# A graph transformer layer with a mixture of experts: factor products paired by weight unit, routed sums carried in PSUM by ScalarE, the second turn moved, and the graph sum split in two parts

## The chip, the cores and the metric

The kernel runs on one core of one Trainium2 chip. The metric is the device time of one execution in microseconds. A core's engines each run their own instructions in a fixed order and meet by semaphores: TensorE (PE) multiplies, VectorE (DVE) and ScalarE (ACT) work element by element, GpSimd (POOL) issues a few gathers, SyncE (SP) issues the loads of the weights.

## The reference, cut to what matters

```python
xn = layernorm(x)                                  # x: 625 x 1024
h = xn @ W; e = exp(-leaky_relu(al[src] + ar[dst]))
gnn = elu(segment_sum(e * h[dst], src) / (segment_sum(e, src) + 1e-5))
mix = linear_attention(xn, w_qkv, w_out, b_out)    # 16 heads, elu + 1 kernel
x = x + gnn + mix
y = layernorm(x)
# 8 experts, top 2, capacity 97 tokens, inner width 4096
eout = (silu(xg @ rg[e]) * (xg @ ru[e])) @ rd[e]   # for each expert e
shared = (silu(y @ sg) * (y @ su)) @ sd            # inner width 8192
x = x + shared + scatter(eout * weight)
```

All is float32.

## The kernel before

Every float32 product is made of three matmuls in the fp32r format: an operand a is split into a_hi (a rounded copy, ScalarE, `hi(u)`) and a_lo = a - a_hi (VectorE, `lo(u)`), and hi*hi, lo*hi and hi*lo are summed in a PSUM bank (`three`). A weight unit is a tile of 128x1024; hi and lo parts of units go round a ring of seven.

A first part (some 480 us) does the edge counts, the layer norm, h, the graph sum (`agg_ps`, in plain float32: 5x5x2 matmuls of the edge weights C by h, with a row sum behind them), Q, K, V, the attention and its output. Then come 32 steps for the experts' layer, four (q=0..3) for each expert e. Each step takes a quarter of the expert's inner width and 1/32 of the shared layer's. The step e=0 q=0 has an order of its own (FIRST), so has e=7 q=3 (LAST); the 30 others are STEP.

A STEP has 35 units. Units 0 to 6 are the factors of a seven-product (Strassen-like) scheme for the shared gate and up weights, in the order A11, S3, S2, A12, S1, A22, S4; S factors are sums of raw blocks that VectorE makes (L1139 to L1149). Each factor is multiplied by tokens in two column tiles j=0, 1 (`product(j, i)`, 12 matmuls of 314 columns). Units 7 to 14 are the routed gate and up weights of half b=0 (`routed_up(0)`), 15 to 18 the shared down weights, 19 to 26 routed half b=1, 27 to 34 the routed down weights (`routed_down(k0, k1)`). The shared down units are multiplied by a seven-product scheme too (`shared_down_products`): P1A, P1B, TA, TB (the last token tile, two triples each), P7A, P7B, P6A, P6B, P2A, P2B, P5A, P5B, P4A, P4B, P3A, P3B, 18 triples in all. They read sh_hi/lo and hs_hi/lo, which are made from the shared inner values: `shared_up`, `shared_mult`, `inner_sums`, `inner_lo`, `inner_sums_lo`; and `down_sums` makes sums of the raw down weights. Partial products that more than one result needs are copied from bank to bank by ScalarE (`down_seed`, L907) and results are added to `resid` by VectorE (`down_add`, L1605).

The routed inner values of half b (`silu_routed(b)` on ScalarE, `routed_inner(b)` on VectorE, L1534, into r_h) are transposed on TensorE (`turn_inner(b)`), split (`turned_hi`, `turned_lo`, L1615) and read by routed_down. The result of a step's eight down units stands in banks R0 and R0+1 and is added to `eout` by VectorE in the next step (`routed_add`, L1493), between the two column tiles' products. At q=0 the next expert's tokens, gathered by GpSimd (`xg`, issued behind the second turn of q=3, since it shares memory with r_h), are transposed (`turn_expert`) and split (`tokens_hi`, `tokens_lo`).

The orders on the engines are written out by hand. ScalarE, GpSimd and SyncE loop over the experts 1 to 6, TensorE and VectorE are unrolled. `kept` and `choice_row` (L1471 to L1483) make the positions and weights for the final sum from the routing.

Of the kernel before, what the change touches and what calls it, by code (L numbers as in the profile page):

```python
# [35 lines left out]
LOW_SBUF = DMA_SCRATCH + 128  # L36
P = 128
# [41 lines left out]
T_BANK = (A0 + 1, A0)  # L79
# [14 lines left out]
AGG_BANK = (7, 0, 1, 2)  # L94
# [24 lines left out]
class Order:  # L119


    def __init__(self, s, gate, sd, rd, a_bank, seq=tuple(range(NPROD)), banks=BANKS, paired=False, sd_units=2):
# [3 lines left out]
        self.down_before, self.after_down = (1, 3) if sd_units == 4 else (0, 1) if s < sd < gate[0] else (None, 0)  # L126
        self.a_bank, self.seq, self.banks, self.paired = a_bank, seq, banks, paired
# [31 lines left out]
    def raw(self, u):  # L159
        if self.shared(u):  # L160
            i = self.seq[u - self.s]
            return SPARE if self.paired and i == F_S2 else self.b0 + FACTOR_RAW[i]
        return self.block(u)
# [7 lines left out]
STEP = Order(s=0, gate=(7, 19), sd=15, rd=27, a_bank=(A0, X0), sd_units=4)  # L171
# [6 lines left out]
def build(nc, x, src, dst, W, a, w_qkv, w_out, b_out, router_w, rg, ru, rd, sg, su, sd, out):  # L178
# [27 lines left out]
    cursor[0] = max(cursor[0], 16512)  # L206
# [149 lines left out]
    assert here() <= early_at  # L356
# [139 lines left out]
    def _(sp):  # L496
# [60 lines left out]
    def _(pool):  # L557
# [15 lines left out]
        link(nc.gpsimd.memset(p7[:], 0.0))  # L573
# [24 lines left out]
        pool.wait_ge(sem("agg_ps"), 2 * NT)  # L598
        nc.gpsimd.memset(vv[:, :, :, P:VW], 1.0).then_inc(sem("v_ones"), 1)
# [50 lines left out]
    def _(act):  # L650
# [94 lines left out]
        for i in range(4):  # L745
            w_part(G_K + 1, i)
        for t in range(NT):
# [3 lines left out]
        for dt in range(NT):  # L751
# [3 lines left out]
            nc.scalar.activation(zt[dt % 2][:], zt[dt % 2][:], ACT.Exp, scale=-1.0).then_inc(sem("ez_done"), 1)  # L755
        for t in range(NT):
# [72 lines left out]
        def step(e, q, order=STEP):  # L829
# [66 lines left out]
            def down_seed(n):  # L896
# [5 lines left out]
                if n in (2, 3):  # L902
                    act.wait_ge(sem("sd_added"), count(e, q, 2 * NT, (2, 1)[n - 2] + ONE))
# [4 lines left out]

            def tokens_hi(half):
                act.wait_ge(sem("xgT_ps"), e * 2 + (half + 1))  # L910
                nc.scalar.copy(xgT_hi[:, half * 4 * CAP:(half + 1) * 4 * CAP],
                               PS[A0 + half][:, 0:4 * CAP]).then_inc(sem("xg_hi"), 1)

            if order is LAST:
                for u in range(15):
# [67 lines left out]
            for u in range(4):  # L983
                hi(u)
            shared_seeds(0, (), (4,), (5,), (6,))
# [3 lines left out]
            shared_seeds(1, (7,), (8,), (9,), (10,), (11, 12), (13,))  # L989
# [1336 lines left out]
```

## Time and profile before

| | |
|---|---|
| median of 3 runs | 2950.28 us (2948.54 to 2950.53) |
| profiled execution | 2947.98 us, of which the span is 2946.2 |
| TensorE busy | 2802.9 us, 95% |
| VectorE busy | 2431.4 us, 83% |
| ScalarE busy | 1659.4 us, 56% |
| TensorE's granted clock, mean | 0.999 of full speed |

The span goes from the first instruction to the last; the rest of the profiled execution's time lies around it. The TensorE clock is given in shares of its full 2.4 GHz. A plain step (q above 0) takes 76.18 us, and an expert of four steps 306.45.

### The profile page before, as it was taken

To read this page: it belongs to the slowest core of one execution; us is meant where nothing else is said; L and a number is where in the kernel's file an instruction comes from. 1 tells how busy PE (TensorE), PEld (TensorE's weight loads), DVE (VectorE), ACT (ScalarE), POOL (GpSimd) and SP (SyncE) were. 2 spreads that over 40 slices of the span, in tenths; PEclk is the share of its full clock that TensorE was granted. 3 is DMA by queue.
4 is the path that set the end of the run, shared out by engine and by line. 5 is a ranking of instruction groups with operands and counts; after the bars stand their busy time and mean duration, and the time that the engine had idled before them with its cause. 6 is when DMAs were issued, how large, how long until landed. Compare 5 with 4: busy or idle time off the path is not lost.

```text
span 2946.2 us, 41411 instructions
## 1 busy us (share of the span) xinstructions
PE 2802.9 (95%) x14706; PEld 2273.9 (77%) x14706; DVE 2431.4 (83%) x3069; ACT 1659.4 (56%) x2271; POOL 57.2 (2%) x74
## 2 busy tenths in 40 slices
PE   9999999999999999999999999999999999999998
PEld 8875898777777777777777777777777777777777
DVE  8756258988888888888888888888888888888888
ACT  7621224555665656655665556655666555556663
POOL 1100000000000000000000000000000000000001
PEclk9999999999999999999999999999999999999999
DMA  3111122666666666665766666666666666666676
GB/s 110 37 57 58 58 72 92 219 207 212 207 212 210 214 212 217 206 213 182 225 208 200 207 219 206 202 206 220 214 208 207 213 204 204 208 219 206 206 247 229
DMA packets 270279, 549.08 MB, mean 186 GB/s; under 512 B 16673, under 2 KB 82465, under 8 KB 269927
## 3 DMA queue, kind: packets, MB, share of 16 engines
q1 hardware_dynamic: 265954, 532.11, 55.7%
q0 software_dynamic: 3936, 14.06, 1.5%
q8 instruction: 117, 1.92, 0.3%
q14 instruction: 110, 0.90, 0.1%
q10 hardware_dynamic: 162, 0.08, 0.0%
HBM read 537.49 MB, written 8.70 MB: 185 GB/s over the span
## 4 chain that ended last, share of the span: by engine, by line
PE 67%; DVE 20%; ACT 6%; issue 5%; DMA 0%; ACTq 0%; DVEq 0%; POOL 0%; POOLq 0%; SPq 0%
PE ps L2042 18%; PE ps L2046 17%; PE ps L2045 17%; DVE c_lo L1508 6%; ACT c_hi L839 4%; PE ps L1810 3%; DVE c_lo L1156 3%; PE ps L1847 2%; PE ps L1849 2%; PE ps L1848 2%; PE ps L1900 1%; DVE raw L1143 1%; DVE raw L1146 1%; DVE raw L1139 1%; ACT c_hi L719 1%
## 5 line engine op out<-in xcount | busy, mean ns | idle before, releaser
L1508 DVE TENSOR_TENSOR c_lo<-raw,c_hi 128x1024 fp32r<-128x1024 f32 x892 | 1054.2, 1217 | 128.4 <-ACT c_hi L839 128.2
L839 ACT CAST c_hi<-raw 128x1024 fp32r<-128x1024 f32 x892 | 894.7, 1047 | 260.5 <-DVE raw L1594 146.9
L2042 PE MATMUL ps<-tok_hi,c_hi 128*128 128x314 f32 x1792 | 558.2, 312 | 51.4 <-DVE c_lo L1156 49.4
L2046 PE MATMUL ps<-tok_hi,c_lo 128*128 128x314 f32 x1792 | 552.0, 308 | 0.0
L2045 PE MATMUL ps<-tok_lo,c_hi 128*128 128x314 f32 x1792 | 552.0, 308 | 0.0
L2042 PE MATMUL ps<-c_hi,xgT_hi 128*97 128x512 f32 x1024 | 406.4, 397 | 0.0
L2046 PE MATMUL ps<-c_hi,xgT_lo 128*97 128x512 f32 x1024 | 403.1, 394 | 0.0
L2045 PE MATMUL ps<-c_lo,xgT_hi 128*97 128x512 f32 x1024 | 402.8, 393 | 0.0
L2042 PEld LDWEIGHTS ps<-tok_hi,c_hi 128*128 128x128 f32 x1792 | 339.3, 189 | 71.4 <-DVE c_lo L1156 43.0
L2045 PEld LDWEIGHTS ps<-tok_lo,c_hi 128*128 128x128 f32 x1792 | 339.8, 190 | 0.1
L2046 PEld LDWEIGHTS ps<-tok_hi,c_lo 128*128 128x128 f32 x1792 | 338.2, 189 | 0.0
L719 ACT CAST c_hi<-raw 128x1024 fp32r<-128x1024 f32 x224 | 230.7, 1046 | 147.8 <-DVE raw L1143 84.0
L1156 DVE TENSOR_TENSOR c_lo<-raw,c_hi 128x1024 fp32r<-128x1024 f32 x224 | 269.8, 1221 | 25.8 <-ACT c_hi L719 24.8
L2042 PE MATMUL ps<-c_hi,hT_hi 128*97 128x512 f32 x512 | 206.4, 403 | 35.1 <-DVE hT_lo L1615 35.1
L2042 PEld LDWEIGHTS ps<-c_hi,xgT_hi 128*97 128x97 f32 x1024 | 166.2, 162 | 73.0 <-issue 9.0
L2046 PEld LDWEIGHTS ps<-c_hi,xgT_lo 128*97 128x97 f32 x1024 | 166.2, 162 | 70.8
L2045 PEld LDWEIGHTS ps<-c_lo,xgT_hi 128*97 128x97 f32 x1024 | 166.3, 162 | 64.2
L2046 PE MATMUL ps<-c_hi,hT_lo 128*97 128x512 f32 x512 | 202.3, 395 | 0.0
L2045 PE MATMUL ps<-c_lo,hT_hi 128*97 128x512 f32 x512 | 201.2, 393 | 0.0
L1605 DVE TENSOR_TENSOR resid<-ps,resid 125x512 f32<-125x512 f32 x300 | 189.1, 676 | 0.0
L883 ACT CAST hT_hi<-ps 128x388 fp32r<-128x388 f32 x64 | 30.6, 478 | 238.0 <-PE ps L2093 238.0
L2042 PEld LDWEIGHTS ps<-c_hi,hT_hi 128*97 128x97 f32 x512 | 82.9, 162 | 86.9 <-DVE hT_lo L1615 42.3
(274 smaller groups left out, 4047.5 us busy)
## 6 DMA issues: line engine op xcount, KB each, us to landing
raw<-in_L_ffn_rg SPq DMA_DIRECT2D x256, 512.0 KB, 4.9
raw<-in_L_ffn_ru SPq DMA_DIRECT2D x256, 512.0 KB, 4.3
raw<-in_L_ffn_rd SPq DMA_DIRECT2D x256, 512.0 KB, 4.8
raw<-in_L_ffn_sg SPq DMA_DIRECT2D x64, 512.0 KB, 5.5
raw<-in_L_ffn_su SPq DMA_DIRECT2D x64, 512.0 KB, 6.3
raw<-in_L_ffn_sd SPq DMA_DIRECT2D x64, 512.0 KB, 4.3
wl<-in_L_mix_w_qkv SPq DMA_DIRECT2D x6, 2048.0 KB, 8.0
wl<-in_L_gnn_W SPq DMA_DIRECT2D x2, 2048.0 KB, 22.2
```

The lines of the kernel that those rows point to most:

```text
L719: nc.scalar.copy(c_hi[u % RING][:], raw_at_(q, r)[:]).then_inc(sem("hi_done"), 1)
L839: nc.scalar.copy(c_hi[u % RING][:], raw_at_(q, r)[:]).then_inc(sem("hi_done"), 1 + (U - order.units) * (u == order.units - 1))
L1156: V.tensor_tensor(c_lo[u % RING][:], raw_at_(q, r)[:], c_hi[u % RING][:].bitcast(F32), ALU.subtract).then_inc(sem("lo_done"), 1)
L1508: V.tensor_tensor(c_lo[u % RING][:], raw_at_(q, r)[:], c_hi[u % RING][:].bitcast(F32), ALU.subtract).then_inc(sem("lo_done"), 1 + (U - ord ...
L1605: V.tensor_tensor(r, PS[bank][0:TP, :], r, ALU.add).then_inc(sem("sd_added"), 1)
L1810: m = MM(PS[dt][0:TP, 0:SC], oh_d[slot(gr, c)][:, dt * TP:(dt + 1) * TP], oh_s[slot(gr, c)][:, 0:SC], start=(c == 0), stop=(c == EG - 1))
L1847: MM(ps, l_hi[:, k, ts], hi[:, i, :], start=(k == 0), stop=False)
L1848: MM(ps, l_hi[:, k, ts], lo[:, i, :], start=False, stop=False)
L1849: m = MM(ps, l_lo[:, k, ts], hi[:, i, :], start=False, stop=(k == KT - 1))
L2042: m = MM(out_, l_hi, r_hi, start=first, stop=False, skip_group_check=skip)
L2045: MM(out_, l_hi, r_lo, start=False, stop=False, skip_group_check=skip)
L2046: return MM(out_, l_lo, r_hi, start=False, stop=last, skip_group_check=skip)
```

## The change

1. STEP's factor products are paired by unit: product(0,i), product(1,i), with four banks for j=1 (R0, R0+1, A0, A0+1). At q=0 the tokens are transposed before the products, and split between them.
2. `routed_add` goes. ScalarE copies the banks into `eout` (`routed_out`) after hi(3), and at q>0 copies `eout` back into the banks (`routed_seed`) after hi(26), so that routed_down sums onto it.
3. The last token tile is treated alike: `last_seed` puts resid into banks 7 and 4, `last_out` takes it out; two VectorE additions go.
4. The hand-written orders of VectorE and ScalarE are changed: `down_sums` and c_lo(15), c_lo(16) stand ahead of `inner_sums_lo`; the down seeds and the additions come earlier among the units; `routed_inner(1)` after lo(32).
5. The second turn comes after two down units instead of four, in bank X0+3.
6. The graph sum uses split operands: 150 matmuls in fp32r instead of 50 in float32, with C_hi and h_hi by ScalarE and C_lo and h_lo by VectorE; a row sum bank, one weight load and a memset are moved for it, and parts of the K and V weights are prepared at other places.
7. `kept` and `choice_row` move from FIRST to the step e=0 q=1, after lo(8).
8. LAST: `routed_out` after hi(5) instead of the additions.

```diff
-T_BANK = (A0 + 1, A0)
+T_BANK = (A0 + 1, X0 + 3)
...
-AGG_BANK = (7, 0, 1, 2)
+AGG_BANK = (7, 6, 1, 2)
+ROWSUM_BANK = 5
...
-STEP = Order(s=0, gate=(7, 19), sd=15, rd=27, a_bank=(A0, X0), sd_units=4)
+STEP = Order(s=0, gate=(7, 19), sd=15, rd=27, a_bank=(A0, X0), banks=((X0, X0 + 1, X0 + 2, X0 + 3), (R0, R0 + 1, A0, A0 + 1)),
+             paired=True, sd_units=4)
...
+        def row_hi(t):
+            act.wait_ge(sem("h_out"), NT + t + 1)
...
+            nc.scalar.copy(h_hi[t][:], h[:, t, :]).then_inc(sem("h_hi_out"), 1)
...
+            def last_seed(half):
+
+                act.wait_ge(sem("sd_added"), count(e, q, 2 * NT, ONE))
+                act.wait_ge(sem("s_up"), count(e, q, 4, 4 + ONE))
+                act.wait_ge(sem("t4_out"), count(e, q, 2, 0))
+                act.wait_ge(sem("silu_done"), count(e, q, 6, 1))
+                nc.scalar.copy(PS[DOWN_LAST[half]][0:TP, :],
+                               resid[:, NT - 1, half * HALF:(half + 1) * HALF]).then_inc(sem("t4_seeded"), 1)
+
+            def last_out(half):
+
+                act.wait_ge(sem("down_ps"), count(e, q, 16, (D_TA, D_TB)[half]))
+                nc.scalar.copy(resid[:, NT - 1, half * HALF:(half + 1) * HALF],
+                               PS[DOWN_LAST[half]][0:TP, :]).then_inc(sem("t4_out"), 1)
+
+            def routed_out(half):
+
+                act.wait_ge(sem("unit_used"), count(e, q, U, USED0))
+                act.wait_ge(sem("eout_clear"), e + (1 if q == 0 else 2))
+                nc.scalar.copy(eout[:, half * HALF:(half + 1) * HALF],
+                               PS[R0 + half][0:CAP, :]).then_inc(sem("rd_added"), 1)
+
+            def routed_seed(half):
+
+                act.wait_ge(sem("rd_added"), count(e, q, 2, half + 1))
+                act.wait_ge(sem("sd_added"), count(e, q, 2 * NT, (6, 8)[half] + ONE))
+                nc.scalar.copy(PS[R0 + half][0:CAP, :],
+                               eout[:, half * HALF:(half + 1) * HALF]).then_inc(sem("eout_seeded"), 1)
...
             if order is LAST:
-                for u in range(15):
+                for u in range(6):
+                    hi(u)
+                routed_out(0)
+                routed_out(1)
+                for u in range(6, 15):
                     hi(u)
...
-            for u in range(4):
-                hi(u)
-            shared_seeds(0, (), (4,), (5,), (6,))
+            hi(0)
+            hi(1)
             if q == 0:
                 tokens_hi(0)
                 tokens_hi(1)
-            shared_seeds(1, (7,), (8,), (9,), (10,), (11, 12), (13,))
+            hi(2)
+            hi(3)
+            routed_out(0)
+            routed_out(1)
...
             inner_sums_hi()
-            for u in range(15, 17):
-                hi(u)
+            hi(15)
+            hi(16)
+            last_seed(0)
+            last_seed(1)
             silu_routed(0)
-            for u in range(17, 22):
-                hi(u)
+            hi(17)
+            hi(18)
             down_seed(0)
             down_seed(1)
-            hi(22)
-            for n in range(2, 6):
-                down_seed(n)
-            for u in range(23, 30):
+            hi(19)
+            last_out(0)
+            last_out(1)
+            down_seed(2)
+            down_seed(3)
+            hi(20)
+            down_seed(4)
+            down_seed(5)
+            for u in range(21, 27):
                 hi(u)
+            if q == 0:
+                act.sem_inc(sem("eout_seeded"), 2)
+            else:
+                routed_seed(0)
+                routed_seed(1)
+            hi(27)
+            hi(28)
+            silu_routed(1)
+            hi(29)
             turned_hi(0)
-            silu_routed(1)
-            for u in range(30, 32):
+            for u in range(30, 35):
                 hi(u)
             turned_hi(1)
...
+            V.tensor_tensor(C_lo[:, dt, :], Cf[:, dt, :], C_hi[dt][:].bitcast(F32),
+                            ALU.subtract).then_inc(sem("C_lo_out"), 1)
...
                 lo(order.s + F_S3)
+                if tokens:
+                    tokens_lo(0)
+                    tokens_lo(1)
                 sums(F_S2)
...
             if order is LAST:
-                for u in range(6):
+                for u in range(15):
                     lo(u)
-                routed_add(count(e, q, U, USED0), cleared)
-                for u in range(6, 15):
-                    lo(u)
...
-                        kept()
-                    if u > 20:
-                        choice_row(u - 21)
...
-            factors()
-            routed_add(count(e, q, U, USED0), cleared)
-            shared_up(0)
-            shared_mult(0)
-            if q == 0:
-                tokens_lo(0)
-                tokens_lo(1)
+            factors(tokens=q == 0)
             for u in range(7, 12):
                 lo(u)
+                if e == 0 and q == 1 and u == 8:
+                    kept()
+                    choice_row(0)
+                    choice_row(1)
+            shared_up(0)
+            lo(12)
             shared_up(1)
-            lo(12)
+            shared_mult(0)
             shared_mult(1)
             inner_sums()
             lo(13)
             inner_lo(0)
             inner_lo(1)
             lo(14)
+            lo(15)
+            lo(16)
+            down_sums()
             inner_sums_lo()
-            for u in range(15, 17):
-                lo(u)
-            down_sums()
+            lo(17)
             routed_inner(0)
-            for u in range(17, 20):
-                lo(u)
-            down_add(DOWN_LAST[0], D_TA, NT - 1, 0)
-            lo(20)
-            down_add(DOWN_LAST[1], D_TB, NT - 1, 1)
+            lo(18)
+            lo(19)
             p7_add(0)
             p7_add(1)
+            lo(20)
+            for p in range(2):
+                down_add(DOWN_B[p], (D_P2A, D_P2B)[p], 2 * p, 0, 1 if p else 3)
             lo(21)
-            for p in range(2):
-                down_add(DOWN_B[p], (D_P2A, D_P2B)[p], 2 * p, 0)
-            lo(22)
             for p in range(2):
                 dve.wait_ge(sem("down_seeded"), count(e, q, 6, 5 + p))
                 down_add(DOWN_A[p], (D_P5A, D_P5B)[p], 2 * p + 1, 1)
+            lo(22)
...
-            for u in range(23, 30):
+            for u in range(23, 29):
                 lo(u)
             turned_lo(0)
+            for u in range(29, 33):
+                lo(u)
             routed_inner(1)
-            for u in range(30, 32):
-                lo(u)
+            lo(33)
+            lo(34)
             turned_lo(1)
...
             for dt in range(NT):
-                m = MM(PS[AGG_BANK[j % 4]][0:TP, :], Cf[:, dt, t * TP:(t + 1) * TP],
-                       h[:, dt, half * HALF:(half + 1) * HALF], start=(dt == 0), stop=(dt == NT - 1))
+                MM(ps, C_hi[dt][:, ts], h_hi[dt][:, cols], start=(dt == 0), stop=False)
+                MM(ps, C_hi[dt][:, ts], h_lo[:, dt, cols], start=False, stop=False)
+                m = MM(ps, C_lo[:, dt, ts], h_hi[dt][:, cols], start=False, stop=(dt == NT - 1))
...
+                seeded = order is STEP and q > 0
...
+                    if k == 0 and seeded:
+                        pe.wait_ge(sem("eout_seeded"), count(e, q, 2, 2))
...
+                    pe.wait_ge(sem("t4_seeded"), count(e, q, 2, half + 1))
...
-            products(0)
             if q == 0:
                 turn_expert()
-            pe.wait_ge(sem("rd_added"), count(e, q, 2, 2))
-            products(1)
+            for i in order.seq:
+                if i == F_S3 and q == 0:
+                    pe.wait_ge(sem("xgT_ready"), e * 2 + 1)
+                product(0, i)
+                if i == F_A11:
+                    pe.wait_ge(sem("rd_added"), count(e, q, 2, 1))
+                if i == F_S3 and q == 0:
+                    pe.wait_ge(sem("xgT_ready"), e * 2 + 2)
+                product(1, i)
...
             turn_inner(0)
             routed_up(1, (1,))
-            routed_down(0, 4)
+            routed_down(0, 2)
             pe.wait_ge(sem("h_done"), count(e, q, 2, 2 + ONE))
             turn_inner(1)
-            routed_down(4, 8)
+            routed_down(2, 8)
```

## Rows read from the trace of the kernel before

**Rows 1.** The page's part 1: busy time, share of the span and instructions.

```profile
PE 2802.9 (95%) x14706; PEld 2273.9 (77%) x14706; DVE 2431.4 (83%) x3069; ACT 1659.4 (56%) x2271; POOL 57.2 (2%) x74
```

**Rows 2.** Waits of TensorE: engine, line, releaser: total us, times, longest.

```profile
PE ps L2042 <- DVE c_lo L1156: 49.4, 58, 1.7
PE ps L2042 <- DVE hT_lo L1615: 35.1, 30, 1.2
PE ps L2042 <- ACT ps L907: 34.7, 30, 1.2
```

**Rows 3.** Windows: us, busy of PE, PEld, DVE, ACT, POOL, clock, DMA share, GB/s.

```profile
2174.77:2250.95 76.18, 72.33 (x374) 58.12 (x375) 65.78 (x75) 45.75 (x60) 0.00 (x0) 1.00 0.64 208
2174.77:2200.82 26.05, 24.74 (x169) 24.49 (x169) 20.30 (x21) 15.09 (x22) 0.00 (x0) 1.00 0.52 168
2211.94:2250.95 39.01, 36.47 (x159) 25.79 (x158) 34.45 (x40) 23.90 (x29) 0.00 (x0) 1.00 0.70 227
481.00:484.00 3.00, 3.00 (x14) 3.00 (x13) 2.22 (x2) 0.83 (x2) 0.00 (x0) 0.51 0.02 6
```

**Rows 4.** Timeline of TensorE in the plain step: start, us, instruction, idle before.

```profile
2179.79 0.38 PE L2042 MATMUL ps<-tok_hi,c_hi 128*128 128x314 f32 x1 [1.31 <-DVE c_lo L1156]
```

**Rows 5.** The page's part 5: busy us, mean ns of one, idle before.

```profile
L1508 DVE TENSOR_TENSOR c_lo<-raw,c_hi 128x1024 fp32r<-128x1024 f32 x892 | 1054.2, 1217 | 128.4 <-ACT c_hi L839 128.2
L839 ACT CAST c_hi<-raw 128x1024 fp32r<-128x1024 f32 x892 | 894.7, 1047 | 260.5 <-DVE raw L1594 146.9
```

**Rows 6.** Timeline of VectorE in the plain step.

```profile
2202.11 0.81 DVE L1552 TENSOR_TENSOR s_up<-s_up,s_gate 128x628 f32<-128x628 f32 x1
...
2214.15 0.68 DVE L1534 TENSOR_TENSOR r_h<-ps,r_h 97x512 f32<-97x512 f32 x1
...
2225.15 3.67 DVE L1605 TENSOR_TENSOR resid<-ps,resid 125x512 f32<-125x512 f32 x6
2228.74 8.02 DVE L1508 TENSOR_TENSOR c_lo<-raw,c_hi 128x1024 fp32r<-128x1024 f32 x7
```

**Rows 7.** Timeline of ScalarE in the plain step.

```profile
2201.02 0.43 ACT L869 ACTIVATE s_gate<-ps 128x314 f32<-128x314 f32 x1 [0.71 <-PE ps L2046]
...
2218.12 1.06 ACT L907 COPY ps<-ps 125x512 f32<-125x512 f32 x2
```

**Rows 8.** Timelines of GpSimd, TensorE, ScalarE and VectorE at the start of e=6.

```profile
2319.95 0.18 POOL L629 COPY tok_cur<-tok_u 97x1 uint32 x1 [277.31 <-PE ps L2093]
2320.97 0.97 POOL L604 DMA_INDIRECT xg<-y_rows,tok_cur  x1 [0.83 <-POOL tok_cur L629]
...
2328.60 0.38 PE L2042 MATMUL ps<-tok_hi,c_hi 128*128 128x314 f32 x1 [1.73 <-DVE c_lo L1156]
...
2342.83 0.87 ACT L911 CAST xgT_hi<-ps 128x388 fp32r<-128x388 f32 x2
...
2343.69 1.02 DVE L1621 TENSOR_TENSOR xgT_lo<-ps,xgT_hi 128x388 fp32r<-128x388 f32 x2
```

**Rows 9.** DMA issues, 2310 to 2340: median us from issue to landing.

```profile
xg<-y_rows,tok_cur POOLq DMA_INDIRECT x1, 8.1
```

**Rows 10.** Groups of TensorE, 236.8 to 281.1: busy us, mean ns of one.

```profile
L1900 PE MATMUL ps<-h,C 125*125 125x512 f32 x100 | 43.3, 593 | 0.0
```

**Rows 11.** Timelines of TensorE and VectorE in FIRST and in LAST.

```profile
542.91 0.18 DVE L1471 TENSOR_SCALAR rt_keep<-rt_rank 125x40 f32<-125x40 f32 x1
...
545.46 0.19 DVE L1477 TENSOR_TENSOR rt_t<-rt_oh,rt_keep 125x40 f32<-125x40 f32 x1
...
550.41 0.55 PE L2093 MATMUL ps<-ident,r_h 97*128 97x97 f32 x4 [2.93 <-DVE r_h L1534]
...
2867.21 1.28 DVE L1493 TENSOR_TENSOR eout<-ps,eout 97x512 f32<-97x512 f32 x2
...
2882.26 0.30 PE L2093 MATMUL ps<-ident,r_h 97*128 97x97 f32 x1 [2.94 <-DVE r_h L1534]
```

**Rows 12.** Timeline of TensorE at the start of FIRST.

```profile
480.25 0.41 PE L2042 MATMUL ps<-tok_hi,c_hi 128*128 128x314 f32 x1 [1.98 <-DVEq L1777]
```

More of the change, by code:

```diff
@@ L36 @@
 LOW_SBUF = DMA_SCRATCH + 128
+RESID_AT = 16512
 P = 128
@@ L161, in raw @@
             i = self.seq[u - self.s]
-            return SPARE if self.paired and i == F_S2 else self.b0 + FACTOR_RAW[i]
+            return SPARE if self.paired and self.sd_units == 2 and i == F_S2 else self.b0 + FACTOR_RAW[i]
         return self.block(u)
@@ L746, in _ @@
             w_part(G_K + 1, i)
+        def row_hi(t):
+            act.wait_ge(sem("h_out"), NT + t + 1)
+            if t == 3:
+                act.wait_ge(sem("biased"), NT)
+            nc.scalar.copy(h_hi[t][:], h[:, t, :]).then_inc(sem("h_hi_out"), 1)
+        for t in range(4):
+            row_hi(t)
         for t in range(NT):
@@ L755, in _ @@
             nc.scalar.activation(zt[dt % 2][:], zt[dt % 2][:], ACT.Exp, scale=-1.0).then_inc(sem("ez_done"), 1)
+        act.wait_ge(sem("w_lo"), w_parts(G_K + 3, 3))
+        act.wait_ge(sem("albc_ps"), 2)
+        for dt in range(NT):
+            act.wait_ge(sem("ez_used"), dt + 1)
+            nc.scalar.copy(C_hi[dt][:], C[:, dt].rearrange("p c two -> p (c two)")).then_inc(sem("C_hi_out"), 1)
+        row_hi(NT - 1)
         for t in range(NT):
@@ L1218, in k_map @@
             feature_map(half * NT + t, ps, TP, HALF, kk[:, t, half * HALF:(half + 1) * HALF])
-            if t < 4:
+            if g is not None and t < 4:
                 w_part(g, t)
@@ L1251, in _ @@
         edge_weights(NT - 1)
-        for t in range(NT):
-            k_map(1, t, G_V)
+        dve.wait_ge(sem("ez_used"), NT)
         csum = zt[1]
@@ L2074, in product @@
                     pe.wait_ge(sem("silu_done"), count(e, q, 6, order.silus(1, 0)))
-                elif i == F_S3 and j == 1:
+                elif i == F_S3 and j == 1 and order is LAST:
                     pe.wait_ge(sem("silu_done"), count(e, q, 6, order.silus(0, 1)))
@@ L2133, in routed_down @@
                         m = three(PS[R0 + half][0:CAP, :], hT_hi[:, xs], hT_lo[:, xs],
-                                  c_hi[u % RING][:, c], c_lo[u % RING][:, c], k == 0, k == 7)
+                                  c_hi[u % RING][:, c], c_lo[u % RING][:, c], k == 0 and not seeded, k == 7, skip=seeded)
                     m.then_inc(sem("unit_used"), 1 + (U - order.units) * (u == order.units - 1))
```

126 lines of the change are left out of this document (91 added, 35 removed).

## The prediction

> **What bounds the kernel now.** I read the page first. TensorE is busy 95% of the span and VectorE 83% [rows 1], so the kernel is near the bound of its matmuls, and what a change of order can win is TensorE's idle time plus matmuls taken away. The list of what TensorE waited for says where that idle time is: three waits that come back in nearly each of the 30 STEP steps, behind a factor's low part (L1156), the seed copies (L907) and the low part of the second turn (L1615) [rows 2]. The windows of one plain step, e=5 q=2 from 2174.77 to 2250.95, give its length, 76.18, split at the starts of routed_up(0) (R, 2200.82) and of the shared down products (D, 2211.94) [rows 3]. The timeline of TensorE puts a number on the first: 1.31 idle before F_S2 [rows 4]; the waits' totals over 30 steps give 1.16 before P6A and 1.17 before the fifth routed_down unit [rows 2]. Counted from start to start, with the slower first matmul after a stall, they cost 1.46, 1.32 and 1.17, with 0.38 at the step's start and 0.15 of small ones: 4.48 a step. TensorE's own work is thus 71.7 and VectorE has 10.4 of slack [rows 3], but both run in a fixed order, so slack in the mean says little. The reader should follow chains.
>
> Durations that I use are pitches: a c_lo shows 1.217 but seven in a row take 8.02, so 1.14 each; six adds take 3.67, so 0.60 each [rows 5, 6]; a c_hi is 1.047, some 0.95 in a row [rows 5]. A product phase of 168 matmuls takes 26.05 less its stalls, 24.2, so one of the 14 products is 1.73 [rows 3]. The 150 matmuls of 512 columns after D, 36.5 of busy time with 8 transposes [rows 3], give 0.233 each, 0.70 for a triple and 1.40 for a routed unit of two.
>
> **Products paired by unit (30 steps).** TensorE now takes 3.46 for a unit's two products. VectorE needs a sum and a c_lo for the next one, 1.2 + 1.14. The stall before F_S2 and that at the start go: the product phase is 24.3 instead of 26.05, 1.8 less. The two additions of routed_add leave VectorE (1.2) and become ScalarE copies behind c_hi(3). Before shows no copy from SBUF to PSUM, and the nearest rows for all new copies are the PSUM-to-PSUM copy of L907, two in 1.06 [rows 7], 0.53 each; twice that is the other bound. I take 0.55. routed_out(0) is then done some 0.3 before product(1,A11) asks for its bank: nothing, but a thin margin. If it is late, it costs its lateness in 23 steps.
>
> **The wait before the shared down products.** This is what the old profile hides. They wait for inner_sums_lo, which in the old order came before c_lo(15), c_lo(16) and the four down_sums. In the new one it comes after all of them. The same instructions, from the multiplication at 2202.11 to the r_h at 2214.15, took 12.04 in an unbroken chain [rows 6]. The new chain starts when the last silu is done, R+0.66 (0.43 of silu after the last product and two hand-overs, [rows 7]), so hs_lo ends at R+12.7 and TensorE starts at about R+12.85, where its 48 matmuls end at R+11.12. A new stall of 1.7.
>
> **Inside the shared down.** P6A's stall goes (last_seed and the seeds move to where ScalarE is free). But down_seed(2) and (3) wait for P6A and P6B, the tenth triple, D+7.0, and c_hi(20) is behind them: ready at D+9.2; c_lo(20) ends at D+10.4, the P2 additions at D+11.6, c_lo(21) and P5A's addition at D+13.4. routed_up(1) needs that addition and wants to start at D+12.6: a stall of 0.75. TA's and TB's additions leave VectorE (1.2); last_seed and last_out (four copies of 0.55) lie on ScalarE, which is busy 45.8 of 76.18.
>
> **Second turn earlier.** turn_inner(1) moves from the fifth to the third unit of routed_down. It needs routed_inner(1), and VectorE has from c_lo(21) on no gap: 12 c_lo (13.6), 6 additions (3.6), hT_lo (0.5) and the multiplication (0.65), 18.4 in all, so from D+11.6 it ends at D+30.0. In the old step the same stretch, six additions from 2225.15 and then seven c_lo, was also unbroken [rows 6]. TensorE wants the turn at D + 12.6 + 0.75 + 11.2 + 0.44 + 2.8 = D+27.8. Stall 2.3 less what the modelled starts hide, 2.2. The old stall of 1.17 before the fifth unit goes.
>
> Sum of a plain step: stalls of 0.07 + 1.7 + 0.75 + 2.2 = 4.7 against 4.48. By ends: R at 24.3, D at R+12.85, the rest 38.95, 76.1; by stalls 76.4. I take +0.1, so +2 over the 23 steps with q>0.
>
> **The steps with q=0 (7).** The tokens of the next expert are gathered by a chain that starts with the second turn of q=3: the copy of the index list at 2319.95, the gather's issue at 2320.97 [rows 8] and its landing 8.1 after that [rows 9], so 9.1 from the copy and, with the turn and the hand-over ahead of the copy, 9.9 from the turn. The new turn is 8.8 before the step's end, the old one about 7.5 (the next step's first product would have been ready at about 2326.7), but the old step used the tokens only after 12 us of products; the new one turns them before its first product. They land 9.9 after D+30.1, 1.1 after the step's end at D+38.9. From the landing X: transposes 0.61, tokens_hi (0.87 for two) and tokens_lo (1.02 for two [rows 8]) to X+2.1, the F_S2 sum behind them to X+3.3, c_hi(2) and c_hi(3) behind that to X+5.2, routed_out(0) to X+5.85, and product(1,A11), ready at X+2.4, waits till X+6.0: 3.5. With the landing, restarts and the first c_lo 5.4 more than work, less the old start stall of such a step, 1.73 [rows 8], which these waits cover: +3.7. Less for the last expert, 1.1. Sum +26. The addition of part 7 to the one step e=0 q=1, 4.46 of VectorE, lies in the slack ahead of the last products, 0 to 1.
>
> **Prologue.** 50 fp32 matmuls, recorded as 100, take 43.3 [rows 10], 44.2 with the row sum. 150 fp32r matmuls of 512 columns at 0.233 and the row sum, 1.0, are 36.1. Their low parts are ready near 232.3, TensorE arrives at 236.89. −8.1; bounds 0 (operands late by so much) and −8.5.
>
> **FIRST and LAST.** The 4.46 of kept and choice rows go (542.91 to 544.32, and two rows of 1.5 such as that from 545.46) from ahead of the r_h whose turn stalls 2.93 in FIRST [rows 11]: −3.1, and −1.1 at the second turn. In LAST the stall is 2.94 behind c_lo, two eout additions (1.28 for two) and four more; the eout additions go [rows 11]: −1.2 at least, −3.7 if both stalls go; I take −2.5.
>
> **Sum.** +2 + 26 − 8.1 − 4.2 − 2.5 = +13. The profiled execution took 2947.98 (span 2946.2), so 2961; the runs' median lies 2.3 above it, so 2963.
>
> **A rule of the clock, weighed.** TensorE's granted clock was 0.51 (the level of 1.2 GHz) in 481.00 to 484.00, right after it had idled 1.98 before 480.25 with transposes ahead; the first products there ran at 0.26 a matmul instead of 0.145, about 1.5 lost [rows 3, 12]. After idles of 2.93 and 2.94 with dense work on either side [rows 11] it did not fall. The Trainium skill ("TensorE: Matmul & The Clock Gate", Part 1) says that idleness puts the array back to 1.2 GHz. By that rule each q=0 step would lose such a stretch again; by the rows at 550.41 it would lose nothing.
>
> **Rivals.** (1) Faster: VectorE's chains are not as tight as I add them up. If the order of arrival lets hs_lo end before R+11.1 (1.7 earlier), 30 steps give −51, 2912; if only the tail chain is shorter by 2.2, −66, 2897; it decides from 0.5 less stall a step on (−15 against +13 gives 2948; 0.7 gives 2942, on the other side). For it: VectorE has 2.4 less to do a step. Against it: the 12.04 was measured. 0.27 with the lower end of my own forecast. (2) The clock falls in the q=0 steps, whose idles of 1.1 and 3.5 are parted by transposes and one product: 7 × 1.5 = +10, 2973. 0.12. (3) The thin margin of routed_out and the seeds fails, a copy at twice its price: 0.5 in 23 steps, +12, 2975. 0.13. (4) Stalls only move and the q=0 wait is half hidden, since the gather lands earlier or ScalarE comes sooner to c_hi(3): +13 − 13, 2950. 0.15 by itself.
>
> **How the numbers follow.** My forecast, 2963, own range 2953 to 2972, has 0.33. A measurement of this kernel tells no change from within 0.2%, 5.9: faster is below 2944.4, slower above 2956.2. Faster takes rival 1, 0.27. Same takes rival 4 and the low end of mine, 0.18. Slower is the rest, 0.55. The range goes down to 2925, which leaves about half of rival 1 out, and up to 2982.
>
> **What would show it.** In a plain step: no gap before F_S2; a gap of 1.5 to 1.9 before the first shared down matmul behind L1583's hs_lo; 0.5 to 1 at the start of routed_up(1); about 2 before the r_h transposes of the second turn, behind r_h; a step of 76.1 to 76.4. In a q=0 step: a gap before the token transposes behind the gather and one of about 3.5 before product(1,A11) behind eout's copy. Aggregation 36 instead of 44. I am wrong if plain steps come out at 75 or less, then at D or at the turn; or if the second gap at q=0 is under 1.

## The result and the profile after

The changed kernel takes 2999.3 us (median of 4 runs, 2997.16 to 3001.31) against 2950.23: 1.0167 of the time before, 95% interval 1.0150 to 1.0185. It is slower, by 49, where 13 were forecast, and lies above the range. The profiled execution took 3001.31, its span is 2999.7.

The page, part 1, and the list of TensorE's waits:

```profile
PE 2816.5 (94%) x14756; PEld 2313.1 (77%) x14756; DVE 2372.0 (79%) x2957; ACT 1799.7 (60%) x2509; POOL 67.8 (2%) x74
```

```profile
PE ps L2163 <- issue: 71.2, 60, 2.0
PE ps L2214 <- DVE r_h L1660: 62.8, 32, 2.1
PE ps L2163 <- ACT eout L960: 20.6, 8, 3.5
PE ps L2225 <- issue: 14.4, 7, 3.2
```

The three waits of [rows 2] are gone, and four others stand there. The first row holds two of them (60 times in 30 steps), which the timeline of TensorE in a plain step (from 949.43) parts:

```profile
986.71 0.48 PE L2163 MATMUL ps<-c_hi,sh_hi 128*125 128x512 f32 x1 [1.62 <-issue]
...
1000.27 0.45 PE L2163 MATMUL ps<-c_hi,xgT_hi 128*97 128x512 f32 x1 [0.74 <-issue]
...
1016.77 0.56 PE L2214 MATMUL ps<-ident,r_h 97*128 97x97 f32 x4 [2.01 <-DVE r_h L1660]
```

From start to start they cost 1.78, 0.90 and 2.18, 4.86 in all, where the prediction had 1.7, 0.75 and 2.2. But two neighbouring steps with the same waits are not equally long. Windows (us, busy time of PE, PEld, DVE, ACT and POOL, TensorE's clock, DMA share, GB/s):

```profile
873.42:949.43 76.01, 71.60 (x376) 58.19 (x375) 61.97 (x69) 49.43 (x68) 0.00 (x0) 1.00 0.63 207
949.43:1027.04 77.61, 73.24 (x376) 59.15 (x375) 65.06 (x73) 51.27 (x70) 0.00 (x0) 0.98 0.61 204
1017.50:1020.50 3.00, 3.00 (x10) 1.92 (x9) 3.00 (x4) 1.29 (x2) 0.00 (x0) 0.55 1.08 369
1113.50:1116.50 3.00, 3.00 (x14) 3.00 (x13) 2.32 (x2) 1.83 (x3) 0.60 (x1) 0.50 0.42 132
```

The first is a step as forecast, 76.01 against 76.18 before [rows 3]. The second is 1.6 longer because TensorE works at half clock for some 3.5 us behind its second turn. The fourth row shows the same at q=0, behind the wait for the old rows' copy. Going through the span in windows of 1 us, and counting busy time by the missing share of the clock, there are 26 such stretches with 43.9 us lost in them; the kernel before has one, with 1.7. Of the 26, 15 come right behind a second turn with 2.0 of idle, 3 behind the wait for the gathered tokens, 7 behind the wait for the old rows' copy and 1 behind the wait for hs_lo.

At q=0 (timelines of GpSimd and TensorE around 1107, and the gather's landing):

```profile
1095.18 1.45 POOL L646 COPY tok_cur<-tok_u 97x1 uint32 x1 [293.68 <-PE ps L2214]
...
1097.47 0.99 POOL L621 DMA_INDIRECT xg<-y_rows,tok_cur  x1 [0.83 <-POOL tok_cur L646]
```

```profile
xg<-y_rows,tok_cur POOLq DMA_INDIRECT x1, 8.6
```

```profile
1106.15 1.19 PE L2225 MATMUL ps<-ident,xg 97*128 97x97 f32 x8 [2.94 <-issue]
```

The copy of the index list takes 1.45 where it took 0.18 [rows 8], and the landing 8.6 instead of 8.1 [rows 9]. So the wait for the gather is 2.94 here, not 1.1; the wait for the old rows' copy is shorter for it, 2.2 in this step and 3.5 in others.

The graph sum is three groups of 50 matmuls where [rows 10] had one of 100 records (groups by line, 215 to 275):

```profile
L2020 PE MATMUL ps<-h_hi,C_hi 125*125 125x512 f32 x50 | 19.8, 395 | 0.0
```

FIRST's first product starts at 470.92 instead of 480.25: 9.3 earlier.

### The profile page after: what moved, and what is told of

Read it like the earlier page. It is cut to its first block, busy times and chain, and to the rows that moved or that the text cites. A ratio compares the mean times of both kernels' runs of the same rounds, so it can differ in the third digit from the quotient of the medians.

```text
span 2999.7 us, 42070 instructions
## 1 busy us (share of the span) xinstructions
PE 2816.5 (94%) x14756; PEld 2313.1 (77%) x14756; DVE 2372.0 (79%) x2957; ACT 1799.7 (60%) x2509; POOL 67.8 (2%) x74
## 4 chain that ended last, share of the span: by engine, by line
PE 73%; DVE 20%; issue 5%; ACT 2%; DMA 0%; ACTq 0%; DVEq 0%; SPq 0%
PE ps L2163 19%; PE ps L2167 19%; PE ps L2166 19%; DVE c_lo L1631 12%; DVE resid L1731 4%; PE ps L1927 3%; PE ps L1964 2%; PE ps L1966 2%; PE ps L1965 2%; ACT c_hi L871 1%; DVE r_h L1660 1%; PE ps L2055 1%; PE ps L2053 1%; PE ps L2054 1%; PE ps L2214 1%
## 5 line engine op out<-in xcount | busy, mean ns | idle before, releaser
L871 ACT CAST c_hi<-raw 128x1024 fp32r<-128x1024 f32 x892 | 912.9, 1048 | 259.3 <-PE ps L2167 80.8
L2163 PE MATMUL ps<-tok_hi,c_hi 128*128 128x314 f32 x1792 | 559.9, 312 | 20.6 <-ACT eout L960 20.6
L2163 PE MATMUL ps<-c_hi,xgT_hi 128*97 128x512 f32 x1024 | 406.6, 397 | 22.1 <-issue 22.1
L736 ACT CAST c_hi<-raw 128x1024 fp32r<-128x1024 f32 x224 | 228.5, 1050 | 152.6 <-DVE raw L1248 65.5
L2163 PE MATMUL ps<-c_hi,hT_hi 128*97 128x512 f32 x512 | 212.6, 415 | 0.0
L2167 PE MATMUL ps<-c_hi,hT_lo 128*97 128x512 f32 x512 | 210.6, 411 | 0.0
L2166 PE MATMUL ps<-c_lo,hT_hi 128*97 128x512 f32 x512 | 210.0, 410 | 0.0
L2163 PE MATMUL ps<-c_hi,sh_hi 128*125 128x512 f32 x340 | 137.7, 405 | 49.6 <-issue 49.0
L939 ACT COPY ps<-ps 125x512 f32<-125x512 f32 x180 | 102.6, 570 | 106.1 <-PE ps L2167 97.6
L890 ACT COPY ps<-ps 128x314 f32<-128x314 f32 x192 | 78.0, 406 | 136.3 <-PE ps L2167 136.2
```

The source lines that it names most:

```text
L736: nc.scalar.copy(c_hi[u % RING][:], raw_at_(q, r)[:]).then_inc(sem("hi_done"), 1)
L871: nc.scalar.copy(c_hi[u % RING][:], raw_at_(q, r)[:]).then_inc(sem("hi_done"), 1 + (U - order.units) * (u == order.units - 1))
L890: nc.scalar.copy(PS[to][:, 0:HW], PS[a][:, 0:HW]).then_inc(sem("seeded"), 1)
L939: nc.scalar.copy(PS[to][0:TP, :], PS[DOWN_A[p]][0:TP, :]).then_inc(sem("down_seeded"), 1)
L2163: m = MM(out_, l_hi, r_hi, start=first, stop=False, skip_group_check=skip)
L2166: MM(out_, l_hi, r_lo, start=False, stop=False, skip_group_check=skip)
```

## The experiments

"Lost" is the busy time lost to the low clock in the profiled execution, summed as above. The step is a plain one without a low stretch. Each ratio is to executions of the kernel before that were timed beside the run; their medians went from 2948.0 to 2950.4, so a difference of two medians below holds to some 2 us. The executions of one kernel with low stretches lie up to 13 apart (x1 2941.4 to 2953.2, x4 2961.2 to 2974.3).

| run | edit, and the kernel it is made on | median us | ratio (95%) | step | lost |
|---|---|---|---|---|---|
| before | | 2950.23 | 1 | 76.15 | 1.7 |
| changed | | 2999.30 | 1.0167 (1.0150 to 1.0185) | 76.02 | 43.9 |
| x1 | hs_lo early, changed | 2945.61 | 0.9994 (0.9984 to 1.0003) | 74.15 | 43.9 |
| x2 | r_h early, changed | 2976.66 | 1.0093 (1.0076 to 1.0110) | 75.9 | 21.5 |
| x3 | idle filled, changed | 2987.08 | 1.0131 (1.0115 to 1.0148) | 76.0 | 25.1 |
| x4 | old rows out first, changed | 2965.73 | 1.0065 (1.0044 to 1.0085) | 76.0 | 30.2 |
| y1 | r_h and hT_lo early, changed | 2990.96 | 1.0135 (1.0118 to 1.0152) | 75.9 | 43.4 |
| y2 | c_hi(20) early, changed | 3000.53 | 1.0173 (1.0156 to 1.0190) | 76.0 | 45.5 |
| y5 | c_hi(20) and (21) early, changed | 2912.99 | 0.9874 (0.9858 to 0.9891) | 73.7 | 26.2 |
| u1 | turn after four, changed | 2979.95 | 1.0093 (1.0076 to 1.0109) | 75.9 | 22.1 |
| b1 | turn after two, before | 2861.92 | 0.9704 (0.9688 to 0.9721) | 73.4 | 4.9 |
| p1 | graph sum alone, before | 2939.15 | 0.9964 (0.9949 to 0.9978) | 76.15 | 1.6 |
| y3 | five edits, changed | 2825.66 | 0.9579 (0.9563 to 0.9595) | 71.9 | 6.8 |
| y4 | five edits, mended, changed | 2783.62 | 0.9435 (0.9419 to 0.9451) | 71.0 | 0 |

### x3: is it the idle that lowers the clock?

```diff
             routed_down(0, 2)
+            for n in range(12):
+                MM(PS[T_BANK[1]][0:CAP, 0:HW], xgT_hi[:, 0:CAP], tok_hi[0][:, n % 4, :], start=True, stop=True)
             pe.wait_ge(sem("h_done"), count(e, q, 2, 2 + ONE))
             turn_inner(1)
```

> The changed kernel with 12 matmuls more, whose result nothing reads, put on TensorE ahead of the wait for the second turn in the 30 STEP steps (1.75 of the 2.01 that it idles there). Nothing else moves. Theory A (the idle is what lowers the clock): no or nearly no low stretch behind plain turns; some 15 of the 25 low stretches at 1.7 each go, 2999 - 25 = 2974. Rival (the falls come from elsewhere, or from any waiting with short transposes): the same 25 low stretches and 2999 or a little more.

The timeline and the windows of a plain step:

```profile
1012.07 1.89 PE L2417 MATMUL ps<-tok_hi,xgT_hi 128*97 128x314 f32 x12
...
1014.30 0.55 PE L2214 MATMUL ps<-ident,r_h 97*128 97x97 f32 x4 [0.34 <-DVE r_h L1660]
```

```profile
949.00:1025.00 76.00, 73.30 (x388) 59.91 (x387) 63.49 (x71) 50.31 (x69) 0.00 (x0) 1.00 0.64 208
1016.00:1019.00 3.00, 3.00 (x15) 2.11 (x14) 3.00 (x4) 1.10 (x2) 0.00 (x0) 1.00 1.07 370
```

r_h comes at the same time, the transposes too, but TensorE has something to do until then: not one of the 15 low stretches behind plain turns is left, and steps are 76.0 where they were 76.0 or 77.6. The work added costs nothing. What is still lost, 25.1, lies at the waits of the q=0 steps, but for one stretch behind a wait for hs_lo. The gain was 12, not 25. A low stretch behind the turn of q=3 (three of the seven in the changed kernel) also stretches the time that the gather has. Without them the gather is waited for 20.6 in all instead of 14.4, and some 6.7 more is lost to the clock at q=0.

### x4 and x1: the two waits that each have one cause

```diff
+            routed_out(0)
+            routed_out(1)
             if q == 0:
                 tokens_hi(0)
                 tokens_hi(1)
             hi(2)
             hi(3)
-            routed_out(0)
-            routed_out(1)
```

> The changed kernel with routed_out(0), routed_out(1) ahead of the tokens' casts and c_hi(2) on ScalarE. Theory A (at q=0 the copy of the old rows is queued behind c_hi(2) and c_hi(3), which wait for a VectorE sum behind the tokens' low parts): the wait before product(1,A11), 2.2 to 3.5, goes in the seven q=0 steps, and with it about half of the low clock stretches there (some 5 x 1.7): 2999 - 20 - 8 = 2971; plain steps unchanged. Rival (S3's products then wait as long for the tokens' low parts): under 5 gained.

34 gained; the wait behind `eout` is gone from the list, and 13.7 less is lost to the clock: 20.6 + 13.7 is 34. Of the 13.7 about 5 is not the edit's: 12 second turns were followed by a low stretch here instead of 15, and nothing around the turn was changed. The plain steps' 76.0 shows that routed_out was never late there.

```diff
+            inner_sums_lo()
             lo(15)
             lo(16)
             down_sums()
-            inner_sums_lo()
```

> The changed kernel with inner_sums_lo put back ahead of c_lo(15), c_lo(16) and down_sums in the STEP steps. Theory A (the order of the changed kernel makes hs_lo late, and VectorE is otherwise in time): the idle of 1.62 before the first shared down matmul (1.78 from start to start) goes in 30 steps, and the clock falls that follow the second turn stay; 2999 - 53 = 2946. Rival (VectorE's chain is tight as a whole): down_sums, c_lo(17) and the chain behind them keep their times, so the 1.78 reappears at the start of routed_up(1) or at the second turn: 2990 or above.

The stall goes in all 30 steps (the first row of the waits, 60 times in the changed kernel, is left with routed_up(1)'s 30) and comes back nowhere: 30 x 1.78 = 53.4, measured 53.7, which is closer than the runs' scatter warrants.

```profile
PE ps L2163 <- issue: 22.1, 30, 0.7
```

The same 43.9 is lost to the clock as in the changed kernel, so the 1.62 of idle before 512-column matmuls had next to no part in that.

### x2, y1, u1: the second turn

```diff
-            for u in range(29, 33):
+            for u in range(29, 31):
                 lo(u)
             routed_inner(1)
+            for u in range(31, 33):
+                lo(u)
             lo(33)
```

> The changed kernel with routed_inner(1) after c_lo(30) instead of c_lo(32). Theory A (the second turn's idle of 2.01 comes from two c_lo ahead of r_h, and that idle, with eight short transposes around it, is also what lowers TensorE's clock to 0.5 about ten times, 1.7 each): the idle goes to under 0.3, and the clock falls behind plain turns go with it: 2999 - 30 x 2.1 - 13 x 1.7 = 2914. Rival (the falls have nothing to do with this idle): only the idle goes, 2936, and the low stretches are as many as before. Second rival (the c_lo behind r_h are then late for the down units): 2960 or more.

The clock part held: 21.5 lost, none of it behind a second turn. The time part did not. TensorE's waits:

```profile
PE ps L2165 <- DVE hT_lo L1741: 50.5, 30, 1.7
PE ps L2227 <- issue: 20.6, 7, 4.1
```

The second rival had named the c_lo behind r_h; what was late is the turn's low part behind four of them. An idle of 1.7 amid 512-column matmuls took the place of one of 2.0 amid transposes, and the clock stayed at 1.00.

y1 has `turned_lo(1)` moved ahead of c_lo(33) and c_lo(34) as well.

> The changed kernel with routed_inner(1) after c_lo(30), as before, and the low part of the second turn (turned_lo(1)) after c_lo(32), ahead of c_lo(33) and c_lo(34). Theory A (with the r_h in time, what was late in the run before was the low part, 1.66 of idle, because four c_lo stood ahead of it): that idle goes too; 2977 - 30 x 1.8 = 2923, with low clock stretches only at q=0. Rival (c_lo(33) and c_lo(34) are then late): an idle of about 1 before the seventh down unit, 2950.

Neither theory had it. The wait moved past the step's end:

```profile
PE ps L2165 <- ACT eout L960: 55.8, 30, 2.5
PE ps L2227 <- issue: 31.6, 7, 5.4
```

The next step's first factor sum (S3, L1244) came no later by VectorE's own count. From c_lo(21), at 998.35 in the changed kernel, VectorE has no gap up to that sum:

```profile
1019.38 1.21 DVE L1244 TENSOR_TENSOR raw<-raw,raw 128x1024 f32<-128x1024 f32 x1
```

That is 21.0, and it is 21.0 in y1 too:

```profile
994.99 1.23 DVE L1631 TENSOR_TENSOR c_lo<-raw,c_hi 128x1024 fp32r<-128x1024 f32 x1 [0.38 <-ACT c_hi L871]
...
1016.01 1.23 DVE L1244 TENSOR_TENSOR raw<-raw,raw 128x1024 f32<-128x1024 f32 x1
```

What changed is that TensorE, without its wait at the turn, is at the next step earlier. There c_hi(2) and c_hi(3) wait for the next sum (S2, 3.7 behind that of S3), and routed_out, queued behind them, misses product(1,A11) by 1.9 in the plain steps too. That is the thin margin of the prediction, and behind that wait the clock was low again in 8 of the plain steps (43.4 lost in all). The stretch of VectorE is 21.0 in x2 and u1 as well, and the plain step 75.9 in all three: the order within the stretch only decides whether TensorE waits for r_h (2.0), for hT_lo (1.7) or for the copy of the old rows (1.9).

u1 undoes part 5 alone (routed_down(0, 4), then the turn).

> The changed kernel with the second turn back after four down units. Theory A (what the moved turn costs here is the order of VectorE, in which r_h is ready at D+30.0): r_h is then in time for a turn at D+30.6, its idle of 2.01 goes, and the wait for the low part, 1.2 to 1.3, comes back as in the kernel before, ahead of which no low clock stretch was seen: 2999 - 30 x 0.9 - 15 x 1.7 = 2947. Rival (the low stretches do not hang on the idle ahead of the transposes): 2972.

19 gained, and the clock gave it (22.1 lost instead of 43.9): the wait for r_h turned into one for hT_lo, which is read right behind this turn and has c_lo(33) and (34) ahead of it on VectorE.

```profile
PE ps L2163 <- DVE hT_lo L1741: 48.7, 30, 1.7
```

The low stretches behind turns went with the wait, as the first theory has it. Its time, 2947, did not come, since it had the new wait at 1.2 to 1.3 and the plain step is 75.9 again.

### y2 and y5: who holds the P additions

In y2 c_hi(20) goes ahead of down_seed(2) and (3); in y5 c_hi(20) and c_hi(21) go ahead of all four seeds.

```diff
             last_out(1)
+            hi(20)
+            hi(21)
             down_seed(2)
             down_seed(3)
-            hi(20)
             down_seed(4)
             down_seed(5)
-            for u in range(21, 27):
+            for u in range(22, 27):
```

> The changed kernel with c_hi(20) ahead of down_seed(2) and down_seed(3) on ScalarE. Theory A (the seeds wait for P6A and P6B, c_hi(20) is queued behind them, and VectorE starves 2.3 for it; that sets the start of the 18.4 us chain up to the second r_h): routed_up(1)'s idle (0.90 from start to start) goes and the chain starts 1.9 earlier, so the second turn's stall falls from 2.18 to 1.1; 30 x 2.0 = 60, and the low clock stretches of the plain steps go with the shorter idle (some 10 x 1.7): 2999 - 60 - 17 = 2922. Rival (the seeds come late for P4 and P3 instead): at most 10 gained.

Nothing moved. VectorE's timeline in the changed kernel, then in y2:

```profile
995.55 1.22 DVE L1631 TENSOR_TENSOR c_lo<-raw,c_hi 128x1024 fp32r<-128x1024 f32 x1 [2.27 <-ACT c_hi L871]
...
998.35 1.23 DVE L1631 TENSOR_TENSOR c_lo<-raw,c_hi 128x1024 fp32r<-128x1024 f32 x1 [0.38 <-ACT c_hi L871]
```

```profile
992.97 1.22 DVE L1631 TENSOR_TENSOR c_lo<-raw,c_hi 128x1024 fp32r<-128x1024 f32 x1
...
998.13 1.23 DVE L1631 TENSOR_TENSOR c_lo<-raw,c_hi 128x1024 fp32r<-128x1024 f32 x1 [2.29 <-ACT c_hi L871]
```

c_lo(20) did come 2.4 earlier (the kernel runs 0.2 ahead), and c_lo(21) starved the 2.3 in its place, at the same time as before, since c_hi(21) was now what stood behind seeds. The rival's number (at most 10 gained) fits, its reason (seeds late for P4 and P3) does not: no such wait is in the list.

> The changed kernel with c_hi(20) and c_hi(21) ahead of the four seeds, nothing else. Theory A (c_hi(21) was the second cork): routed_up(1)'s 0.90 goes, P5A's addition ends about 1.5 earlier, and with TensorE 0.9 earlier the second turn's stall falls from 2.18 to about 1.6: 2999 - 30 x 1.5 = 2954, less 0 to 25 for low clock stretches that a shorter idle avoids. Rival (something else than ScalarE's queue holds c_lo(20) and c_lo(21)): 2999.

With both moved, 86 are gained, 70 of it in the stalls (2.35 a step) and 18 in the clock.

```profile
PE ps L2215 <- DVE r_h L1661: 21.8, 32, 1.2
```

The wait for r_h has fallen from 2.0 to 0.7 and the one at routed_up(1) is gone. More than forecast: VectorE's stretch of 21.0 starts earlier by the 2.3 that VectorE had starved, and the step is shorter by as much.

### b1 and p1: parts of the change on the kernel before

```diff
-            routed_down(0, 4)
+            routed_down(0, 2)
             pe.wait_ge(sem("h_done"), count(e, q, 2, 2 + ONE))
             turn_inner(1)
-            routed_down(4, 8)
+            routed_down(2, 8)
```

> The kernel before the change with one edit, the second turn after two down units instead of four; its VectorE order is kept, in which r_h is ready before the third unit. Theory A (the move of the turn is good by itself and costs only where r_h is late for it): the wait for the low part, 1.17 of idle in 30 steps, goes and no idle replaces it: 2948 - 35 = 2913. Rival (the move itself is bad, since r_h or the low part is late there too): 2948 or more.

87 gained, not 35. In the list of waits [rows 2]'s one for hT_lo is gone, and the one behind the factor's low part has fallen from 49.4 to 21.6:

```profile
PE ps L2042 <- ACT ps L907: 34.8, 30, 1.2
PE ps L2042 <- DVE c_lo L1156: 21.6, 31, 1.3
```

The earlier turn also frees VectorE from waiting for it, so that it reaches the next step's factors sooner: its idle time before hT_lo is 17.9 in all in b1 and 101.9 before. In the timeline of the kernel before:

```profile
2244.10 0.56 DVE L1615 TENSOR_TENSOR hT_lo<-ps,hT_hi 128x388 fp32r<-128x388 f32 x1 [3.41 <-ACT hT_hi L883]
```

The two waits make 63 of the 87; the plain step is 2.8 shorter, 2.0 of it idle time, and the rest is not parted. The move of the turn is thus worth 87 on the old order and, with r_h late, was ahead of 15 low stretches on the new one.

b1 shows one thing more. Its FIRST is that of the kernel before, with the same idle of 2.93 before the turn that [rows 11] has at 550.41, and this time the clock fell behind it; the windows are of b1 and then of the kernel before:

```profile
549.47 0.56 PE L2093 MATMUL ps<-ident,r_h 97*128 97x97 f32 x4 [2.93 <-DVE r_h L1534]
```

```profile
551.00:554.00 3.00, 3.00 (x9) 1.99 (x8) 3.00 (x4) 1.54 (x2) 0.49 (x1) 0.50 0.75 225
551.00:554.00 3.00, 3.00 (x14) 2.11 (x13) 3.00 (x4) 2.65 (x4) 0.95 (x1) 1.00 0.58 183
```

In p1 the idle of 2.95 in LAST, whose order is also that of before, was followed by 0.50 too (2873.43 to 2876.85). So neither the length of an idle nor the work beside it settles whether the clock falls; what does stays open.

> The kernel before the change with the prologue's part alone: split operands and 150 fp32r matmuls for the graph sum, the row sum's bank, the moved weight load, memset and weight parts. Both theories: FIRST starts 9.3 earlier, as in the changed kernel, and the steps keep their 76.15: 2948.5 - 9.3 = 2939. If the operands of the experts' steps were disturbed by it, less would be left.

11 gained by the medians against 9.3 foreseen, 8.5 by the profiled spans; FIRST starts at 471.79 in it, 8.5 earlier than before, and the steps are as long as they were.

### y3 and y4: all mends together

> The changed kernel with all edits together: inner_sums_lo ahead of c_lo(15), c_hi(20) ahead of the seeds, routed_inner(1) after c_lo(30) and turned_lo(1) after c_lo(32), routed_out ahead of the tokens, and the tokens' transposes after product(0,A11). Theory A (each wait is the end of a chain of its own, and nothing shared by them is full): stalls of 4.86 a step become about 0.3, at q=0 one wait of 1.3 for the gather is left, no low clock stretch after FIRST: 2999 - 30 x 4.5 - 7 x 5 - 42 = 2787. Rival (VectorE, with 63 of then 71.5 us, or the loads bound the step): plain steps of 73 or more, 2830 or above.

> The kernel with all edits, but c_hi(20) and c_hi(21) both ahead of the four seeds, and the tokens' transposes after both products of A11. Theory A (with c_hi(20) alone moved, c_hi(21) stood in its place behind down_seed(4) and (5), which wait for P5; with both moved VectorE does not starve): the 0.90 at the start of routed_up(1) goes in 30 steps, and the gather has 1.75 more, of 2.0 that it was waited for, with about 1 of waiting for the tokens' split in its place; 2826 - 27 - 6 = 2793, a plain step of 71.0. Rival (the seeds come late for P4 and P3, or the split costs what the gather gave): 2815 or above.

y3 has the edits of x1, x4, y1 and y2, and `turn_expert()` after product(0,A11). y4 has y5's order of the seeds in place of y2's, and `turn_expert()` after both products of A11. The page of y4 and two of its plain steps:

```profile
PE 2757.3 (99%) x14756; PEld 2290.0 (82%) x14756; DVE 2357.2 (85%) x2957; ACT 1776.4 (64%) x2509; POOL 62.5 (2%) x74
```

```profile
839.88:910.79 70.91, 70.91 (x375) 58.44 (x374) 63.12 (x71) 49.56 (x68) 0.00 (x0) 1.00 0.68 225
910.79:981.93 71.14, 71.14 (x375) 58.37 (x374) 63.07 (x71) 49.55 (x68) 0.00 (x0) 1.00 0.68 221
```

y3 came out 39 above its first theory's 2787: routed_up(1)'s 0.74 was left (22.1), the gather was waited for 14.2, and 6.8 went to the clock. y4, forecast at 2793, took 2784. TensorE has no idle time left in its two plain steps and no low stretch while it works. y4 is 5.6% faster than the kernel before, so the change with these mends is worth 167; how much of that is the paired products' or the copies' on ScalarE was not parted (the moved turn alone gave 87 on the old order).

## Why the prediction was wrong

**The plain steps: right.** Stalls of 1.7, 0.75 and 2.2 were forecast and 1.78, 0.90 and 2.18 came; a step took 76.02 where +0.1 on 76.18 was taken. x1, y5 and x2 confirm the causes of the three: the order of hs_lo, the copies ahead of c_hi(20) and c_hi(21), and the chain up to r_h. One step of the working was incomplete: the prediction named c_hi(20) alone as what starves VectorE, and y2 shows that c_hi(21) behind the next two seeds sets the chain's start as well.

**The steps with q=0: right in mechanism, one term too small.** The wait for the copy of the old rows was forecast at 3.5 and is 3.5 at most, 20.6 in all; the wait for the gather was put at 1.1 and is 2.1 in the mean (14.4 over 7) and 2.94 in the step shown, since "9.1 from the copy" took the copy at 0.18. It takes 1.45 in six of the seven and 0.31 in one. The two waits together are 5.0 a step where the prediction had 4.6. (In its sum, 7 x 3.7 less the 1.1 of the last expert is 25, not 26; that changes nothing.)

What the copy's time hangs on can be read from the runs, though none was made for it. In the kernel before, p1 and b1 VectorE has nothing running at that point, and all 21 copies take 0.18. In the other eleven kernels the copy starts while VectorE subtracts one c_lo after the other, and each of the 77 copies ends 0.04 to 0.05 behind the end of a c_lo, the last before the row runs out: 0.35 in y4 and 0.85 to 0.88 in u1, where hT_lo is next, 1.45 in most, 3.7 in x2, where three more c_lo follow. The 0.31 is at a place where the next c_lo started 0.01 before the end of the last and not 0.08. GpSimd and VectorE at one of x2's:

```profile
1398.36 3.72 POOL L646 COPY tok_cur<-tok_u 97x1 uint32 x1 [288.02 <-PE ps L2216]
```

```profile
1397.41 4.63 DVE L1631 TENSOR_TENSOR c_lo<-raw,c_hi 128x1024 fp32r<-128x1024 f32 x4
1401.95 0.57 DVE L1741 TENSOR_TENSOR hT_lo<-ps,hT_hi 128x388 fp32r<-128x388 f32 x1
```

The Trainium skill ("GPSIMD Engine Reference", Specifications) names contention for SBUF with VectorE instructions that have two SBUF inputs, as c_lo has; the traces agree, with 3.72 beside a row of c_lo and 0.18 beside an idle VectorE.

**The clock: the step that failed.** The sum has no term for it: the prediction weighed it only as a rival for the q=0 steps, 7 x 1.5, at a chance of 0.12, since "by the rows at 550.41 it would lose nothing". It lost 43.9. Of that some 25 is behind 15 of the 30 plain second turns, an idle of 2.0 whose effect on the clock the prediction never asked about, though it had forecast that idle itself; 10 stretches, some 17, are in the q=0 steps. The kernel before had three such idles on record: one of 1.98 was followed by the low clock, two of 2.93 and 2.94 were not [rows 11, 12]. The prediction took the two for the rule. b1 and p1 show that they were none: the same two idles were followed by 0.50 there. As an estimate from those rows, one in three of the 37 long idles that the prediction itself had laid out (30 turns, and 7 waits of 3.5), at its 1.5 each, would have been +18, 2981; all of them +55, 3018. The measured time lies between, and the half that came could not be known from before.

The Trainium skill ("TensorE: Matmul & The Clock Gate", Part 1) has the array fall back to 1.2 GHz when it idles. The trace agrees, 0.50 to 0.55 in the windows above, and x3 shows it by filling the idle; but half of the second turns' idles of 2.0 were followed by no fall.

**Ledger by span**, 53.5 longer: start of FIRST −9.3, FIRST −6.0 (forecast −4.2, and 1.7 of it is the low stretch that it had before), LAST −2.7 (forecast −2.5), the 30 STEP steps +71.6. Of these 43.9 is the clock and 27.7 the rest, for which the forecast had 28. Without the low stretches in either kernel the change would have been +11, beside a forecast of +13. The prologue gave 9.3 for 8.1; p1, with its part alone, 8.5. Where the other 0.8 comes from stays open.

**Rivals.** (2) had the true cause, for the wrong places and far too cheap: its 10.5 at q=0 was some 17, and the 15 stretches behind the plain turns it did not have. (3)'s thin margin did not bind in the changed kernel (x4 leaves plain steps at 76.0) but did as soon as the turn was mended (y1). (1), a looser chain, did not occur, nor (4): the gather came later, not earlier.

## What to carry to other kernels

When a forecast holds a new idle on TensorE of 1.5 to 3 us next to small matmuls or transposes, price the half clock that may follow it, about 1.7 a time, in each place where it stands, and not only where the old trace has shown it. Before a wait is mended, ask what sets the start of the chain that it ends. The three waits that x2, y1 and u1 traded for one another hung on one stretch of VectorE, and the plain step stayed at 75.9 until y5 let that stretch start earlier; y2, which moved one of the two copies that held it, gained nothing. Waits with chains of their own add up: x1, x4, y5 and y1 alone gave 54 + 34 + 86 + 8 = 182, all together, with the gathered tokens' transposes moved as well, 216. Test each part of a change on the old order too: the moved turn alone was worth 87.

## What the runs showed of the hardware that was not expected

- Which idles were followed by the low clock in the changed kernel: 15 of the 30 idles of 2.0 before the transposes of the second turn, and all 7 of 1.9 to 3.5 before product(1,A11), but before the shared down matmuls only the one of 1.98 and none of the 29 of 1.62, and none of the 30 of 1.64 to 1.72 ahead of the first matmul that reads hT_lo in x2. An idle of 2.93 in FIRST was followed by it in b1 and not in the kernel before. A stretch costs 1.6 to 1.7 each time.
- A one-column GpSimd copy of 97 rows takes 0.18 beside an idle VectorE. Started beside an unbroken row of c_lo, it ends 0.04 to 0.05 behind the row's last (up to 3.72 in x2), and a VectorE instruction that reads a PSUM bank (hT_lo) ends the row for it. The gather behind it lands 7.6 to 9.5 after its issue in the steps e=1 to 7 of the changed kernel.
- ScalarE's copies from SBUF to PSUM, which no row of before showed, take 0.55 (two in 1.10, L967), as the 512-column copy between banks does (two in 1.06, [rows 7]).
